# Softmax stage of a one-core transformer block: 64-row TensorE tiles, two-bank slots for the stream of row maxima, and another order of heads

## The reference, cut to what matters

```python
b, l, d = x.shape                  # 4, 1024, 256; 16 heads of 16
q, k, v = split(x @ W_qkv.T + b_qkv)
scores = einsum('bqhe,bkhe->bhqk', q, k) / sqrt(16)
scores = where(tril(ones(l, l)), scores, -inf)
attn = softmax(scores, axis=-1)
out = einsum('bhqk,bkhe->bqhe', attn, v)
```

## Time and profile before

| | |
|---|---|
| median of three runs | 1540.11 us (1534.96 to 1540.85) |
| profiled execution, its own time | 1542.46 us |
| span of its trace | 1540.8 us |
| softmax_stage, from its first memset to its last PV | 502.4 to about 1099 us |
| one group in steady state | 33.68 us |

### The profile page before, as it was taken

How to read it: one execution, slowest core, us unless ns; L and a number is a source line. 1 busy time by engine, 2 the same in 40 slices (tenths; PEclk the granted TensorE clock), 3 DMA queues, 4 the chain that set the end, 5 groups by cost and what they waited for, 6 DMA issues and landing times. The chain is left out here.

```text
span 1540.8 us, 31184 instructions
## 1 busy us (share of the span) xinstructions
PE 1325.7 (86%) x8678; PEld 1003.7 (65%) x8709; DVE 1019.6 (66%) x2335; ACT 775.6 (50%) x1949; POOL 496.9 (32%) x651
## 2 busy tenths in 40 slices
PE   2628999899699499999998999999778269998998
PEld 1417999799588255555555555554465159997998
DVE  6594555499866777767675777773286755554787
ACT  2524556333244046666675666666546236564333
POOL 1554444255300201222211112212324554443454
PEclk9658999899899569999998999999896569999999
DMA  6503434122465712223322222200315114433233
GB/s 188 169 3 97 123 123 122 60 73 74 146 233 231 136 30 43 44 43 66 61 44 44 43 43 43 44 2 1 114 35 167 55 59 124 123 123 93 83 112 106
DMA packets 86509, 135.73 MB, mean 88 GB/s; under 512 B 12992, under 2 KB 66176, under 8 KB 83328
## 3 DMA queue, kind: packets, MB, share of 16 engines
q1 hardware_dynamic: 64896, 90.29, 22.1%
q0 software_dynamic: 13056, 35.67, 8.3%
q10 hardware_dynamic: 8448, 8.39, 1.6%
HBM read 81.35 MB, written 52.43 MB: 87 GB/s over the span
## 5 line engine op out<-in xcount | busy, mean ns | idle before, releaser
L1448 DVE TENSOR_REDUCE s_MX<-s_ps_a 128x1 f32<-128x512 f32 (+4 forms) x624 | 368.9, 643 | 133.8 <-PE s_ps_a L1515 132.2
L1422 ACT ACTIVATE s_PR<-s_ps_b 128x512 f32<-128x512 f32 (+3 forms) x768 | 343.7, 491 | 162.3 <-PE s_ps_b L1537 155.2
L1515 PE MATMUL s_ps_a<-s_KO,s_QO 96*128 96x512 f32 (+3 forms) x768 | 286.1, 422 | 22.7 <-DMA s_QO<-qk_scratch 22.7
L1537 PE MATMUL s_ps_b<-s_QO,s_KO 98*128 98x512 f32 (+3 forms) x768 | 266.6, 368 | 7.2 <-issue 3.9
L1391 POOL TENSOR_SCALAR_AFFINE_SELECT s_PR<-s_PR 128x256 f32<-128x256 f32 x256 | 103.5, 407 | 474.5 <-ACT s_PR L1422 473.6
L1537 PEld LDWEIGHTS s_ps_b<-s_QO,s_KO 98*128 98x128 f32 x768 | 146.3, 194 | 72.6 <-ACT s_PR L1422 54.4
L603 POOL DMA_INDIRECT f_XG<-xn_scratch,f_tok_u x144 | 136.4, 947 | 167.3 <-PE f_ps_x L700 157.4
L1515 PEld LDWEIGHTS s_ps_a<-s_KO,s_QO 96*128 96x128 f32 x768 | 152.1, 211 | 28.7 <-DVE s_MX L1448 20.8
L810 POOL DMA_INDIRECT f_YG<-y_scratch,f_slots_u x128 | 121.0, 945 | 150.2 <-DVE X L885 94.6
L1552 PE MATMUL s_ps_o<-s_PR,s_VG 128*17 128x512 f32 (+3 forms) x1536 | 163.0, 496 | 5.3 <-POOL s_PR L1391 5.3
L656 DVE TENSOR_TENSOR f_xl<-f_ps_x,f_xh 128x256 fp32r<-128x256 f32 x144 | 61.1, 425 | 97.7 <-ACT f_xh L628 92.6
(11 more groups left out here) (206 smaller groups left out, 2966.9 us busy)
## 6 DMA issues: line engine op xcount, KB each, us to landing
y_scratch<-f_YS SPq DMA_DIRECT2D x144, 128.0 KB
s_KO<-qk_scratch SPq DMA_DIRECT2D x48, 256.0 KB, 5.8
s_QO<-qk_scratch SPq DMA_DIRECT2D x96, 128.0 KB, 6.6
xn_scratch<-f_XN ACTq DMA_DIRECT2D x16, 512.0 KB, 3.2
qk_scratch<-p_QKh SPq DMA_DIRECT2D x32, 256.0 KB
qk_scratch<-p_QKl SPq DMA_DIRECT2D x32, 256.0 KB
f_stage<-in_w_up SPq DMA_DIRECT2D x20, 352.0 KB
X<-in_x SPq DMA_DIRECT2D x4, 1024.0 KB, 9.4
```

The lines of the kernel that those rows point to most:

```text
L1422: nc.scalar.activation(PR[:, u // 2 % SLOTS, u % 2, 0:W - lo], ps_b[u % RING][:, lo:W], ACT.Exp, scale=SCALE).then_inc(exp_done, 1)
L1448: nc.vector.tensor_reduce(MX[:, h:h + heads, i, s], ps_a[v % RING][:, 0:heads * keys].rearrange("p (h n) -> p h n", h=heads), AX.X, ALU.ma ...
L1515: last = nc.tensor.matmul(ps_a[v % RING][:, at:at + keys], QO[k][0:R, h, i * P:(i + 1) * P], KO[k][0:R, h % 2, s * W:s * W + keys], start= ...
L1537: nc.tensor.matmul(ps_b[u % RING][:, lo:W], KO[k][0:RM, h % 2, i * P:(i + 1) * P], QO[k][0:RM, h, hf * W + lo:(hf + 1) * W], start=True, s ...
```

## The change

- A head has its own 48 rows (50 with the maxima), and two heads lie in one tile of 128 rows: heads 0 and 2 on partitions from 0, heads 1 and 3 on partitions from 64. No zeros are needed in QO. The loads of a group are 12 DMAs where there were 9; the maxima are placed by 4 DMAs where there were 2.
- A unit covers two heads (or four) at once: `ps_a` is two slots of two banks each. The matmul of the lower 64-row tile writes the first bank, that of the upper tile the second, and one tensor_reduce reads both. There are 21 units a group where there were 39. The mask of a diagonal unit is four bf16 matmuls over 64 rows where there was one over 128.
- The bank `ps_t` is gone: the transposes take a slot of `ps_a` in their turn. The order of uses of a slot is written in USES; each use waits until the use two before it has been read (one semaphore, `slot_read`). turn_output and turn_max come after the second head of their step, where they came after the fourth head and PV. VectorE takes one A unit of that step, then normalise or max_low, then the step's other units.
- The heads of B go in the order 0, 2, 1, 3, with one semaphore for each half of the rows. The matmuls of B have 50 rows where they had 98.

Worked out from the new lists: 3, 2, 1, 1, 2, 2, 2, 3, 2, 2, 1, 0 units beside steps 0 to 11, MAX_T = 8, OUT_T = 7. The unit split in two is one with 256 keys (i = 5).

```diff
-    R = 3 * PH
+    R = 3 * HD
     RM = R + 2
+    TILE = P // 2
...
-            wide = W // keys
+            wide = min(W // keys, 2)
+            A_UNITS += [(i, s, hp, wide, keys) for hp in range(0, 2, wide)]
...
+    for n in range(NB):
+        beside = [("a",) + one for one in A_BESIDE[n]]
+        USES += beside[:1]
+        if n == 1:
+            USES.append(("out", -1, 1))
+        if n == OUT_T:
+            USES.append(("out", 0, 0))
+        if n == MAX_T:
+            USES.append(("max", 1, 0))
+        USES += beside[1:]
...
+    HEAD_ORDER = (0, 2, 1, 3)
...
-        ps_a = [ps(f"ps_a{i}", [P, W]) for i in range(RING)]
+        ps_a = [ps(f"ps_a{i}", [P, 2, W]) for i in range(2)]
...
-        ps_t = ps("ps_t", [P, W])
...
             def place_max(g):
...
+                    for c in range(2):
+                        row = c * TILE + R + r
+                        sp.dma_start(QO[k][row:row + 1, :, :].bitcast(F32),
+                                     src[c * 2 * NQ:(c + 1) * 2 * NQ, :].bitcast(F32)).then_inc(max_rows[k], 16)
...
         def _(dve):
-            nc.vector.memset(QO[0][0:RM, :, :].bitcast(F32), 0.0).then_inc(zeros[0], 1)
-            nc.vector.memset(KO[0][R:RM, :, :].bitcast(F32), 1.0).then_inc(ones, 1)
+            for k in range(4):
+
+                for c in range(2):
+                    rows = slice(c * TILE + 32, (c + 1) * TILE)
+                    nc.vector.memset(KO[k][rows, :, :].bitcast(F32), 1.0).then_inc(ones, 1)
...
+                    for c in range(2):
+                        dve.wait_ge(a_done[c], NA * g + v + 1)
+                    _, slot = slot_of_a(g, v)
+                    scores = ps_a[slot][:, :, 0:heads * keys].rearrange("p c (h n) -> p c h n", h=heads)
+                    nc.vector.tensor_reduce(MX[:, :, hp:hp + heads, i, s], scores, AX.X,
+                                            ALU.max).then_inc(slot_read, 1)
...
+                    if not isinstance(g, int) or q >= 2:
+                        pe.wait_ge(slot_read, q - 1)
                     if diagonal:
...
+                        for j in range(2):
+                            for c in range(2):
+                                rows = slice(c * TILE, (c + 1) * TILE)
+                                scores = banks[c][:, 0:heads * keys].rearrange("p (h n) -> p h n", h=heads)
+                                nc.tensor.matmul(scores[:, :, keys - P + j * TILE:keys], identb[rows, j, :],
+                                                 neg[rows, 0:heads, 0:P - j * TILE],
+                                                 start=j == 0, stop=False, skip_group_check=True)
+                    for hp in range(hp0, hp0 + heads):
+                        at = (hp - hp0) * keys
+                        for c in range(2):
+                            rows = slice(c * TILE, c * TILE + R)
+                            last = nc.tensor.matmul(banks[c][:, at:at + keys], QO[k][rows, hp, i * P:(i + 1) * P],
+                                                    KO[k][rows, hp, s * W:s * W + keys], start=not diagonal,
+                                                    stop=True, skip_group_check=True)
...
             def turn_output(g, hf):
+                q, slot = out_slot(g, hf)
                 pe.wait_ge(o_copied, 2 * g + hf + 1)
...
+                pe.wait_ge(slot_read, q - 1)
...
-                        if h == GH - 1:
-                            if n >= 1:
-                                pv_step(g, k, n - 1)
+                        if h == 1:
                             if n == 1 and since(g, 1):
                                 turn_output(g - 1, 1)
-                            if n == MAX_T - 1:
+                            if n == OUT_T:
                                 turn_output(g, 0)
                             if n == MAX_T and until(g, 1, NG):
                                 turn_max(g + 1)
+                        if h == GH - 1 and n >= 1:
+                            pv_step(g, k, n - 1)
```

More of the change, by code:

```diff
@@ L1258, in softmax_stage, with slot_use, slot_of_a @@
     MAX_T = 1 + max(n for n in range(NB) if (1, NA - 1) in A_BESIDE[n])
+    OUT_T = MAX_T - 1
+    USES = []
+    for n in range(NB):
[8 more added lines that the diff above has]
+        USES += beside[1:]
+    NU = len(USES)
+    FIRST = NA + 1 + AHEAD
+    def slot_use(g, what, ahead, index=0):
+        at = USES.index((what, ahead, index))
+        if not isinstance(g, int):
+            return FIRST - 1 + NU * g + at, (FIRST - 1 + at) % 2
+        q = FIRST + sum(0 <= n + use[1] < NG for n in range(g + 1) for use in USES[:at if n == g else NU])
+        return q, q % 2
+    def slot_of_a(g, v):
+        if isinstance(g, int) and g * NA + v < NA + AHEAD:
+            q = v + g * (NA + 1)
+            return q, q % 2
+        ahead = 1 if v >= AHEAD else 2
+        return slot_use(g - ahead, "a", ahead, v)
+    HEAD_ORDER = (0, 2, 1, 3)
     SLOTS = 6
-    LOAD = 9 * 16
-    PLACE = 2 * 16
-    assert GH == 4 and D // G == 64 and GH * NB % RING == 0 and NB * 2 % SLOTS == 0 and MAX_T < NB
+    LOAD = 12 * 16
+    PLACE = 4 * 16
+    assert GH == 4 and D // G == 64 and GH * NB % RING == 0 and NB * 2 % SLOTS == 0 and MAX_T < NB and NU % 2 == 0
+    assert all(len(A_BESIDE[n]) <= GH for n in (1, OUT_T, MAX_T))
     with ExitStack() as c:
@@ L1493, in _ @@
                         max_low(g + 1)
+                    for groups, v in A_BESIDE[n][1:]:
+                        a_beside(g, groups, v)
             normalise(NG - 1, 3, 1)
@@ L1507, in a_units @@
                     if diagonal:
-                        scores = ps_a[v % RING][:, 0:heads * keys].rearrange("p (h n) -> p h n", h=heads)
-                        nc.tensor.matmul(scores[:, :, keys - P:keys], identb[:, :], neg[:, 0:heads, :],
-                                         start=True, stop=False, skip_group_check=True)
-                    for h in range(h0, h0 + heads):
-                        at = (h - h0) * keys
-                        last = nc.tensor.matmul(ps_a[v % RING][:, at:at + keys], QO[k][0:R, h, i * P:(i + 1) * P],
-                                                KO[k][0:R, h % 2, s * W:s * W + keys], start=not diagonal,
-                                                stop=True, skip_group_check=True)
```

171 lines of the change are left out of this document (82 added, 89 removed).

## The result

The changed kernel took 1696.55 us (median of four runs, 1693.78 to 1705.98), the kernel before 1540.48 (four runs, 1534.96 to 1543.17). The ratio is 1.1029, 95% interval 1.0974 to 1.1084: slower, as forecast, but by 156 us and not by 23. The profiled execution took 1699.01 us, with a span of 1697.3.

The account below looks back on a forecast made before the run. TensorE's queue was taken to bound the kernel: from 1542.46 us profiled, +26 for slot waits and -2.5 at the stage's start gave 1566, less 2.4 to the median scale: 1563 us. Range 1515 to 1598, the forecast's own 1550 to 1580.

Parts of the forecast that it names:

- the granted clock: TensorE's clock in the middle of the softmax stage, expected to stay near 1.00.
- C: Rival: waiting lowers TensorE's clock, one 1.2 GHz spell a group, about +1.6 us each, 1586 us in all; chance 0.10.
- the sum: Step times of one group added up with waits: 35.5 us against 33.68, +1.8 a group, +26 us over 14.3 groups.
- the walk: Step-by-step timing of a group by starts of PV, with slot waits of 4.7 us within 35.5 us.
- steps 0 and 1: From PV(11) to PV(0): TensorE waits for slots to be read; 6.4 us against 4.88 before, plus 1.5.
- step 7: From PV(5) to PV(6): units and output transposes wait for slots; 5.4 us against 4.13 before, plus 1.3.
- The pair: Two A matmuls on separate row tiles run at once: 0.25 us at 512 columns, 0.22 at 384 and less.
- B: Rival: pairs of matmuls on row tiles don't overlap, 5.8 us more a group, about 1624 us; chance 0.06.
- The reduce: VectorE's read of both banks, 1024 elements, takes 1.22 us, or 1.13 back to back.
- A: Rival: one reduce reads both banks at once in 0.69 us, giving 1514 us; chance 0.21 for both its forms.
- Head order and 64-row loads: B's new head order and 64-row weight loads might remove cold starts of matmuls; put at nothing.
- The start of the stage: First maximum stream, bound by VectorE: fewer, longer reads and no zeroing of QO save 2.5 us, bounds 0 and 5.

Follow-up runs that it names:

- aft_64: Changed kernel with A and B contracted over all 64 rows of their tile instead of 48 and 50; 1590.16 us, ratio 1.0372.
- bef_ring2: Kernel before with two banks in the ring of A instead of three, rows as before; 1588.30 us, ratio 1.0361.
- aft_b114: Changed kernel with the matmuls of B over 114 rows, A still in pairs of 48 rows; 1617.93 us, ratio 1.0555.
- aft_ab114: Changed kernel with B over 114 rows and A over 112, so no pairs overlap; 1625.05 us, ratio 1.0599.
- bef_rows50: Kernel before with A over 48 rows and B over 50 instead of 96 and 98; 1938.61 us, the shorter of two runs.
- aft_late: Changed kernel with transposes, normalise and max_low behind a step's A units, transposes also behind PV; 1600.05 us, ratio 1.0442.
- aft_ol: Changed kernel with head order 0, 1, 2, 3 and late transposes, still 48 and 50 rows; 1551.32 us, the shorter of two runs.
- aft_64o: Changed kernel with A and B over 64 rows and head order 0, 1, 2, 3; 1561.82 us, ratio 1.0192.
- aft_64ol: Changed kernel with 64 rows, head order 0, 1, 2, 3 and late transposes; 1536.44 us, ratio 1.0033.

## Why the prediction was wrong, point by point

**The step that failed** is the granted clock. The prediction held it near 1.00 in every group of its sum, and put its fall among the rivals as C, for spells of waiting, at +1.6 us a group and a chance of 1 in 10. It was 0.70, and a group took some 43 us. At full clock the group is 34.7 us, in aft_64 and in the changed kernel itself (772.89 to 807.59), so of the 145.0 us before the last group about 14 are the schedule's (14.3 x 1.0). A second idle spell (below) is 4.4, and the rest, some 126, goes with the clock. Another 10.5 are the last group's, at a clock of 0.53 for 0.89, which the sum had left as it was. C had the right sign; a group lost some 8 us to the clock (43.1 - 34.7, less the spell), five times its 1.6, for two reasons.

- *What it made of the cause.* C argued from waits, and found those of 0.4 to 0.7 us shorter than what B leaves idle without A. Its rows say otherwise: the wait shown there is 0.21 us, and the whole last group idles for 30.75 - 27.99 = 2.8 us, less than the 4.7 that the walk gave every group. But waits by themselves are not enough: bef_ring2, aft_b114 and aft_ab114 wait three to five times as long as the kernel before and hold 0.98. Rows are: bef_rows50 fell to 0.55 without any wait. The order of the work matters as well: at the same 48 and 50 rows, late transposes brought the clock from 0.70 to 0.81, and with the other order of heads to 0.92. Whether this comes through waits is open. In a group at full clock TensorE was idle for 4.5 us in the changed kernel, 2.9 in aft_late and 3.1 in aft_ol, which speaks for it; against it, with 64 rows the kernel that idles most, aft_64o (5.1 a group), has the highest clock of its kind, 0.97.
- *What it took for a spell.* One PV and four B at 1.2 GHz in a group. A mean of 0.70 between 0.50 and 1.00 means 60% of the time at 1.2 GHz; of the three windows of 5 us shown, one is wholly slow and one wholly fast.

The rows of before held a hint, that in its last group, without A units, the clock is 0.89; no row had a matmul over fewer than 96 rows beside a clock, so the price itself was not to be read there. A fair upper bound for such an unknown is the whole stage at 1.2 GHz, and the range of the forecast left it out.

The Trainium skill (TensorE: Matmul & The Clock Gate, A second HAM failure mode: psum-queue depth-cycling) says that short idle spells of TensorE, as it goes round its PSUM banks, made the clock swing between its two levels in another kernel. The trace shows the swing, but agrees with that cause only in part: with 96 to 114 rows such spells left the clock at 0.98.

**The walk held.** In aft_64's group at full clock, by starts of PV: steps 0 and 1 6.28 us (6.4 forecast), step 2 2.15 (2.15), steps 3 to 5 6.48 (6.5), step 6 2.59 (2.72), step 7 5.15 (5.4), step 8 3.90 (4.1), steps 9 to 12 8.11 (8.24). Together 34.66 for 35.5. So the change costs 1.0 us a group at full clock, where 1.8 were forecast: the sign holds, the size is about half. The starts, from the timeline of TensorE in aft_64:

```profile
744.31 0.41 PE L1621 MATMUL s_ps_o<-s_PR,s_VG 128*17 128x128 f32 x8 [0.28 <-POOL s_PR L1437]
750.59 1.05 PE L1621 MATMUL s_ps_o<-s_PR,s_VG 128*17 128x512 f32 x8
752.74 0.84 PE L1621 MATMUL s_ps_o<-s_PR,s_VG 128*17 128x384 f32 x8
...
759.22 1.05 PE L1621 MATMUL s_ps_o<-s_PR,s_VG 128*17 128x512 f32 x8
761.81 1.05 PE L1621 MATMUL s_ps_o<-s_PR,s_VG 128*17 128x512 f32 x8
766.96 1.05 PE L1621 MATMUL s_ps_o<-s_PR,s_VG 128*17 128x512 f32 x8
770.86 1.05 PE L1621 MATMUL s_ps_o<-s_PR,s_VG 128*17 128x512 f32 x8
...
778.97 0.41 PE L1621 MATMUL s_ps_o<-s_PR,s_VG 128*17 128x128 f32 x8 [0.28 <-POOL s_PR L1437]
```

The changed kernel's own group at full clock has the same steps to 0.02 us each. TensorE's idle time is 34.67 - 30.17 = 4.5 us in the one and 34.70 - 30.20 = 4.5 in the other; 4.7 were forecast.

**The pair** runs at once, as taken, so B falls. Its price was too low and that of two B too high: in aft_64 a pair and the two B after it (512 and 384 columns) take 0.34 and 0.26 us, where the walk's prices give 0.25 and 0.42 (0.235 and 0.18). That the two errors partly cancel in the sum is luck. The timeline of TensorE in aft_64:

```profile
746.79 0.50 PE L1581 MATMUL s_ps_a<-s_KO,s_QO 64*128 64x512 f32 x2 [0.72 <-DVE s_MX L1503]
747.13 0.39 PE L1605 MATMUL s_ps_b<-s_QO,s_KO 64*128 64x512 f32 x2
747.39 0.50 PE L1581 MATMUL s_ps_a<-s_KO,s_QO 64*128 64x512 f32 x2
747.73 0.34 PE L1605 MATMUL s_ps_b<-s_QO,s_KO 64*128 64x384 f32 x1
```

Two matmuls of B on different tiles overlap too, which the walk did not have.

**The reduce** over two banks took 1222 ns; 1.22 us was forecast, so A falls: the banks are not read at once. VectorE was busy for 23.4 us a group, as forecast.

**Head order and 64-row loads**, put at nothing: wrong for the order, 28 us with 64 rows and 46 in the changed kernel. The loads were not tried by themselves.

**The start of the stage**: -1.7 us, forecast -2.5.

**What stays open.** The effect of rows is shown at 48 and 50, 64, 66 and from 96 on, not how the chip comes to it: neither whether it is the rows that a matmul contracts or the part of the array that it takes, nor why head order and the transposes' place move the clock too. Why aft_64ol, with its shorter group, stays at 0.95 is open as well, and so is what would hold it at 1.00. Not tried were the idle spells in the steady stage that end with nothing the profile shows. The kernel before has one of 3.9 us; the changed kernel has two, with one matmul of B between them, and so has every kernel made from it. The timeline of TensorE, before and after:

```profile
831.39 0.79 PE L1537 MATMUL s_ps_b<-s_QO,s_KO 98*128 98x512 f32 x1 [3.93 <-issue]
```

```profile
903.24 0.79 PE L1595 MATMUL s_ps_b<-s_QO,s_KO 50*128 50x512 f32 x1 [3.84 <-issue]
908.40 0.80 PE L1571 MATMUL s_ps_a<-s_KO,s_QO 48*128 48x512 f32 x2 [4.38 <-issue]
```

The second costs 4.4 us, which the prediction had nowhere.

## What to carry to other kernels

Before matmuls are moved to smaller tiles of the array, price the granted clock: run the kernel as it is with only the rows cut down, and read the clock of the stage. Here that one edit cost some 400 us, more than any wait or any overlap could win. It is a warning and not a forecast: with the same rows the clock was 0.55 there, 0.70 in the changed kernel and 0.92 in aft_ol. Where row tiles are used all the same, fill them (64 rows for 48 and 50: 101 us here, 15 to 43 with the other order and late transposes), let neighbours in the queue stand on different tiles, and keep an operation that needs a slot behind the units that are ready.

## What the runs showed of the hardware that was not expected

- With the same instructions and no waits, matmuls over 48 and 50 rows ran at a granted clock of 0.55, over 66 rows at 0.91, over 96 and 98 rows at 0.99. After the same idle spell the clock came back in 10.2 us with 96 and 98 rows and in 71.7 with 66. Half of the 96 rows of before meet zeros in QO, and so do the rows that aft_64 adds, so rows that meet zeros count as well.
- TensorE idle for 9% of the time with 112 and 114 rows: clock 0.98. Idle for 10% with 48 and 50: 0.70.
- Going from a 114-row matmul to a pair on 64-row tiles costs about 0.2 us and back about 0.1 (estimate from starts 0.42 and 0.43 apart, less 0.235 for B and 0.34 for a pair).
- The columns occupied by PV, 17 or 32 of each tile, left clock and time as they were.
